# Routing, token lists and tile plan moved into the first shared half of the feed-forward, and a low part moved from VectorE to GpSimd

## The reference

```python
kv = einsum('bhil,bhjl->bijhl', k_, v_)
y = irfft(rfft(kv, n=2L) * rfft(ssm_kernel, n=2L))[..., :L]
out = einsum('bijhl,bhil->bjhl', y + kv * D, q_)
x = x + out
```

```python
scores = sigmoid(x @ router_w)                # 32 experts
group_scores = top-2 sum of (scores + bias) in each of 8 groups
keep 4 groups, take the top 8 experts; weights = scores / sum * 2.5
routed = sum over the 8 experts of w * (silu(x@gate) * (x@up)) @ down     # inner 512
shared = (silu(x @ sw_gate) * (x @ sw_up)) @ sw_down                      # inner 1024
out = x + routed + shared
```

## Time and profile before

| | us |
|---|---|
| median of 3 runs | 13680.2 (13676.1 to 13680.58) |
| profiled execution | 13610.97 |
| its span | 13609.1 |
| TensorE busy in the span | 13142.6 |

### The profile page before, as it was taken

How to read it: one execution, slowest core, us unless ns; L and a number is a source line. 1 busy time by engine, 2 the same in 40 slices (tenths; PEclk the granted TensorE clock), 3 DMA queues, 4 the chain that set the end, 5 groups by cost and what they waited for, 6 DMA issues and landing times.

```text
span 13609.1 us, 192445 instructions
## 1 busy us (share of the span) xinstructions
PE 13142.6 (97%) x59424; PEld 10914.0 (80%) x59425; DVE 5798.7 (43%) x6513; ACT 3143.2 (23%) x4072; POOL 6330.1 (47%) x6629
## 2 busy tenths in 40 slices
PE   8999995999999999999999999999898999999999
PEld 7888884888888888877888887877787888888887
DVE  6888785333333333343333333333334333333333
ACT  4444442111122111222122212222222112112111
POOL 5688886111444444444444444444444444444111
PEclk9999997999999999999999999999999999999999
DMA  3333333444444444455455545555555444444444
GB/s 120 118 115 111 115 115 91 135 128 127 113 114 110 103 107 104 115 146 127 98 114 132 115 97 127 125 135 142 141 115 159 98 97 114 97 97 103 128 128 120
DMA packets 876587, 1597.96 MB, mean 117 GB/s; under 512 B 169537, under 2 KB 518081, under 8 KB 850306
## 3 DMA queue, kind: packets, MB, share of 16 engines
q0 software_dynamic: 258560, 642.82, 23.1%
q1 hardware_dynamic: 134018, 600.31, 13.2%
q10 hardware_dynamic: 483840, 352.54, 10.4%
HBM read 995.66 MB, written 599.86 MB: 117 GB/s over the span
## 4 chain that ended last, share of the span: by engine, by line
PE 76%; DMA 2%; DVE 2%; issue 1%; ACT 1%; ACTq 0%; DVEq 0%; SPq 0%; POOL 0%
PE gps L1274 26%; PE ups L1274 26%; PE yps L1274 25%; DMA hsd<-hb 1%; DVE wlo L1199 1%; DMA hz<-hsd 1%; DMA raw<-in_w_gu_dram 0%; ACT whi L1143 0%; ACT xhi L1149 0%; DVE xlo L1199 0%; DVEq L991 0%; ACTq L1155 0%; DVE hp L1232 0%; ACTq L991 0%; DVE hb L1234 0%
## 5 line engine op out<-in xcount | busy, mean ns | idle before, releaser
L1112 POOL DMA_INDIRECT x2d<-yrow,yidx x544 | 945.7, 1738 | 3837.2 <-issue 1581.8
L1076 POOL DMA_INDIRECT xg<-xnd,xidx x2176 | 2156.7, 991 | 969.0 <-issue 473.2
L1199 DVE TENSOR_TENSOR xlo<-xt,xhi 128x1024 fp32r<-128x1024 f32 x672 | 822.5, 1224 | 3792.3 <-ACT xhi L1149 3792.3
L1274 PE MATMUL gps<-whi,xhi 128*128 128x512 f32 x5376 | 2098.2, 390 | 211.4 <-DVE xlo L1199 119.1
L1274 PE MATMUL ups<-whi,xhi 128*128 128x512 f32 x5376 | 2094.1, 390 | 0.0
L1274 PE MATMUL gps<-wlo,xhi 128*128 128x512 f32 x5376 | 2093.7, 389 | 0.0
L1274 PE MATMUL ups<-wlo,xhi 128*128 128x512 f32 x5376 | 2093.4, 389 | 0.0
L1274 PE MATMUL gps<-whi,xlo 128*128 128x512 f32 x5376 | 2093.3, 389 | 0.0
L1274 PE MATMUL ups<-whi,xlo 128*128 128x512 f32 x5376 | 2093.1, 389 | 0.0
L1274 PE MATMUL yps<-whi,hhi 128*128 128x512 f32 x5376 | 1667.6, 391 | 124.4 <-DVE wlo L1199 116.7
L1274 PE MATMUL yps<-wlo,hhi 128*128 128x512 f32 x5376 | 1662.3, 390 | 0.0
(11 more groups left out here) (149 smaller groups left out, 17382.3 us busy)
## 6 DMA issues: line engine op xcount, KB each, us to landing
hsd<-hb ACTq DMA_DIRECT2D x2688, 64.0 KB
hz<-hsd ACTq DMA_DIRECT2D x672, 256.0 KB, 2.7
raw<-in_w_gu_dram SPq DMA_DIRECT2D x136, 1024.0 KB, 7.2
raw<-in_w_dn_dram SPq DMA_DIRECT2D x68, 1024.0 KB, 6.9
xg<-xnd POOLq DMA_DIRECT2D x512, 128.0 KB
yrow<-x2d SPq DMA_DIRECT2D x128, 512.0 KB, 3.4
kT<-in_ctx_dram SPq DMA_DIRECT2D x64, 704.0 KB, 8.1
xg<-xnd,xidx POOLq DMA_INDIRECT x2176
```

Source lines behind the costliest of these rows:

```text
L1076: pool.indirect_dma_start(out=xg[i][:, q, :], out_offset=None, in_=quarters, in_offset=bass.IndirectOffsetOnAxis(ap=xidx[i][:, q:q + 1], a ...
L1112: pool.indirect_dma_start(out=acc, in_=yrow[i][:, :], in_offset=None, out_offset=bass.IndirectOffsetOnAxis(ap=yidx[i][:, 0:1], axis=0), co ...
L1199: return dve.tensor_tensor(dst, src, hi.bitcast(F32), ALU.subtract)
L1274: ins = pe.matmul(ps, rows, w[:, chunk, i * 512:(i + 1) * 512], start=first and n == 0, stop=last_one and n == 2)
```

## The change

- The routing leaves the mixing stage. `mix` keeps only the logits: ScalarE copies them into `lg`, 128 x 64 x 32, which stays in SBUF with `con` and `biasb`. `plan` is gone.
- In the mixing stage GpSimd makes the low part of group 3 as well, right after that of group 2; VectorE's `last_kv_lower` is gone. `xres` has two buffers.
- The feed-forward block begins right after mixing. Its SP loads the first x rows, the first weights, more x rows, and then goes through the first shared half with `pass_on`: x rows of the tile 3 ahead, store, wait, fetch. GpSimd loads no x rows in this half.
- ScalarE makes one sigmoid of all logits (128 x 2048) after the first weights are split.
- The 64 shared tiles are walked by `walk_routing` (tiles 0 and 1, then 8 rounds of 6 tiles, then tiles 50 to 59) and `walk_rest`. Each of a round's 6 tiles does one piece of routing on VectorE: `choose_groups`, `choose`, `weigh`, `count`, `assign`, `hand_over`. The piece stands between the addition to `yrow` and `hlo`. TensorE's two `ranks` matmuls stand in the third tile of the round, between gate/up and down. `plan_tiles` is the piece of tile 50.
- `assign` and `hand_over` fill the list entries in halves of 4 tiles (`match_half`). `assign` waits before its half for `place_free`, which GpSimd gives when the lists of the round before have landed.
- GpSimd goes through the 8 rounds of lists by itself, waiting for `placed` of each.

The diff, cut to its core:

```diff
-        xres = sb("xres", [P, L])
+        xres = [sb(f"xres{i}", [P, L]) for i in range(2)]
...
                 kv_lower(s, 2)
-                if isinstance(s.block, int) and s.block == BLOCKS - 1:
-                    list_tokens(s.block - 2, (2 * s.u, 2 * s.u + 1))
-                elif s.u < 7 and routes(s, s.u, 2):
-                    list_tokens(s.block - 2, ((0,), (1,), (2,), (3,), (4,), (5,), (6, 7))[s.u])
-                elif routes(s, 7, 2):
-                    free_place(s.block - 2)
+                kv_lower(s, 3)
...
-            def last_kv_lower(s):
...
-                if routes(s, 6, 1):
-                    count(s.block - 1)
...
-                if routes(s, 7, 1):
-                    assign(s.block - 1)
...
-                if g < GROUPS - 1:
-                    pe.wait_ge(kv_low, (GROUPS - 1) * n + g + 1)
-                else:
-                    pe.wait_ge(kv_low_last, n + 1)
+                pe.wait_ge(kv_low, GROUPS * n + g + 1)
...
-def plan(nc, A, keep):
...
+ROUNDS, PIECES, RANKS = NTILE // RB, 6, 2
+PLANNED = 2 + ROUNDS * PIECES
...
+def walk_routing(eng, tile, chain=None):
+
+
     for t in range(2):
         tile(Tile(t))
...
+    with eng.Fori(0, ROUNDS) as rnd:
+        if chain:
+            chain.restart(eng)
+        for u in range(PIECES):
+            tile(Tile(2, u, rnd * (PIECES // 2), rnd, u))
...
+    tile(Tile(PLANNED, piece=PIECES))
+    tile(Tile(PLANNED + 1))
+    pairs(eng, tile, PLANNED + 2, R0 - 4)
...
+            def pass_on(store, stored, first, end, ahead=0):
+
+                with sp.Fori(0, (end - first) // 2) as turn:
                     for i in range(2):
...
+                        n = first + 2 * turn + i
+                        if ahead:
+                            load_rows(n + ahead, (i + ahead) % 2)
+                        store(n, i)
+                        sp.wait_ge(stored[i], 16 * (first // 2 + turn + 1))
+                        fetch(n + 2, i)
...
+            load_rows(0, 0)
+            load_weights(sp, raw, w_ld, *expert_weights(A, 0), lambda unit: None)
+            load_rows(1, 1)
...
+            pool.sem_inc(place_free, 1)
+            with pool.Fori(0, ROUNDS) as rnd:
+                pool.wait_ge(placed, rnd + 1)
+                settle(pool, pool_turns)
+                for t in range(RB):
+                    list_tile(pool, lists, pair, place, t, listed)
+                pool.wait_ge(listed, 16 * RB * K * (rnd + 1))
+                pool.sem_inc(place_free, 1)
...
+            act.activation(lg[:, :, :], lg[:, :, :], ACT.Sigmoid).then_inc(scored, 1)
...
+                for t in range(RB):
+                    last = dve.max(top[:, t, :], key[:, t, :])
+                link(last)
+
+                dve.wait_ge(place_free, r + 1)
+                match_half(0)
...
+                if c.piece is not None:
+                    (choose_groups, choose, weigh, count, assign, hand_over, plan_tiles)[c.piece](c.rnd)
                 if c.on():
                     dve.wait_ge(h_hi, t + 1)
                     low(hlo[:, :, :].rearrange("p k (q s) -> p q k s", s=SQ), hz[:, :, :, :],
                         hhi[:, :, :].rearrange("p k (q s) -> p q k s", s=SQ)).then_inc(h_lo, 1)
...
+                if c.piece == RANKS:
+                    pe.wait_ge(chose, c.rnd + 1)
```

More of the change, by code:

```diff
@@ L240, in mix_and_route @@
         sd_out = sb("sd_out", [P, 3])
[L241 to L259, removed]
+        lg, con, biasb = keep["lg"], keep["con"], keep["biasb"]
         ident = con[:, C_ID:C_ID + P]
@@ L339, in step @@
                 if s.on(OUT):
-                    wait(sp, x2_st, 16 * s.n(OUT))
-                    sp.dma_start(xres[:, :], head_rows(x, s.n(OUT))).then_inc(r_ld, 16)
+                    i = s.slot(OUT)
+                    wait(sp, x2_st[i], 16 * s.half(OUT))
+                    sp.dma_start(xres[i][:, :], head_rows(x, s.n(OUT))).then_inc(r_ld[i], 16)
                 if s.on(FETCH):
@@ L700, in _ @@
             walk(dve, step, seq)
-            choose_groups(NTILE // RB - 1)
-            choose(NTILE // RB - 1)
-            count(NTILE // RB - 1)
-            assign(NTILE // RB - 1)
         @block.tensor
@@ L1044, in _ @@
                 sp.wait_ge(y_st[i], 16 * EXPERT_TILES // 2)
-            sums(store_sum, out_st)
+            for i in range(2):
+                fetch(i, i)
+            pass_on(store_sum, out_st, 0, NTILE - 2)
+            for i in range(2):
+                store_sum(NTILE - 2 + i, i)
             for i in range(2):
@@ L1118, in tile @@
                     load_list(c, 3)
-                if c.on(2):
+                if c.on(2) and c.part(2) != 0:
                     bring(c, 2)
@@ new lines, in choose @@
+            def choose(r):
+                link(dve.tensor_scalar(msk[:, :, :], msk[:, :, :], 0.0, None, ALU.add))
+                for t in range(RB):
+                    last = dve.max(top[:, t, :], msk[:, t, :])
+                link(last)
+                for t in range(RB):
+                    last = dve.match_replace(rep[:, t, :], top[:, t, :], msk[:, t, :], -3e38)
+                link(last)
+                dve.tensor_tensor(chosen[:, :, :], rep[:, :, :], msk[:, :, :], ALU.not_equal)\
+                    .then_inc(chose, 1)
+                dve.wait_ge(chose, r + 1)
@@ L1256, in tile @@
                     new_weights(dve, c, 0, split_dn)
-            for q in range(QUADS):
-                last = dve.tensor_copy(quad[:, q:q + 1], quarter[:, :])
-            last.then_inc(quad_ready, 1)
             x_turn(Tile(0), 0)
@@ L1264, in _ @@
             x_turn(Tile(0), 1)
-            walk_tiles(dve, tile)
+            for q in range(QUADS):
+                last = dve.tensor_copy(quad[:, q:q + 1], con[:, C_QUAD:C_QUAD + 1])
+            last.then_inc(quad_ready, 1)
+            dve.memset(cnt[:, :], 0.0)
+            dve.tensor_copy(tokf[:, :], con[:, C_TOK:C_TOK + RB])
+            walk_routing(dve, tile, seq)
+            dve.wait_ge(tab_ld, 16)
+            walk_rest(dve, tile)
         @block.tensor
```

450 lines of the change are left out of this document (204 added, 246 removed).

## The result

The changed kernel takes 13947.39 us (median of 4 runs, 13938.39 to 13958.61), the kernel before 13680.39 in the same session (4 runs, 13676.1 to 13695.64): 1.0194 times, interval 1.0176 to 1.0211. Forecast were 13540 us. It is 267 us slower instead of 140 faster, and outside of every rival's case.

What follows compares the result with a forecast made beforehand. TensorE, busy 97% of the span, was taken to bound the kernel. Mixing -69, start of feed-forward -109, ranks matmuls +7 and wait for lists +31 gave -140 us, from 13680.2 to 13540, range 13495 to 13600.

Steps and rivals of the forecast that it cites:

- What bounds the kernel: Whole kernel: TensorE bounds it, busy 97% of the span; in mixing it loses 14.1 us per eight heads to routing.
- Mixing without routing: Mixing stage, heads 8 to 62: without routing each head takes 32.63 us, a gain of 69 us.
- The low part on GpSimd: Mixing stage: the added 2.70 us a head hides in over 10 us of GpSimd's idle time; cost 0.
- From mixing to the first tile: Start of feed-forward: first matmul comes 23 us after the barrier instead of at 2365.9, a gain of 109 us.
- Pieces of routing, ranks matmuls: First shared half: VectorE's pieces fit in 8.7 us of room, cost 0; the ranks matmuls cost TensorE 7 us.
- The wait for the lists: First shared half: VectorE waits 6.7 us in assign for GpSimd's lists, costing TensorE 4.4 us in seven rounds, 31 us.
- The upper bound, 165 us in all: Wait for the lists at most: GpSimd's round takes 97.5 us, TensorE idles 14.4 us a round, plus 9.2 of clock.
- The exclusion by VectorE, the third case: Long stall in the shared half: VectorE's exclusion or late landings make GpSimd's round 91 us or more; 13593 to 13674; chance 0.24.
- no room before `hlo`: Shared half: routing pieces stand wholly on TensorE's path, 248 us with clock, giving 13757 us; chance 0.04.
- these 69 us: Profiled execution against the median of runs: the median is 69 us above, and the same difference was assumed after the change.
- 13509: Rival without a stall in the shared half: lists land in time, -171 us, giving 13509 us; chance 0.19.

Runs made afterwards that it cites:

- e1: The changed kernel without its 512 list transfers, so lists stay blank and routed tiles compute with other rows; 13435.03 us.
- e7: The kernel before with only the last low part of each head moved from VectorE to GpSimd; 13720.11 us, ratio 1.0031.
- e12: The changed kernel with each round's 64 indirect list transfers replaced by 64 plain GpSimd transfers of the same pieces to fixed rows; 13513.68 us.
- e17: The changed kernel without h's way through HBM in all tiles, and without row loads and yrow's store and fetch in the first shared half; 13847.19 us.
- e9: The changed kernel with each of the 512 list transfers making 16 writes instead of 128; 14000.16 us.
- e15: The changed kernel with room for four rounds' places and shares, rounds written out, and a GpSimd pause after every second list transfer; 13551.23 us, ratio 0.991.

## Why the prediction was wrong, by its steps

*What bounds the kernel.* Right: `e1`, with all pieces in the shared half, keeps TensorE busy 1207.11 of 1210 us.

*Mixing without routing.* Right, if 5 us short: heads 8 to 62 take 2135.94 - 368.94 = 1767.0 us, forecast 1762.0; a gain of 64.2 for 69.2.

```profile
368.94 1.21 DVE L521 TENSOR_TENSOR xres<-xres,ps 128x1024 f32<-128x1024 f32 x1
...
2135.94 1.21 DVE L521 TENSOR_TENSOR xres<-xres,ps 128x1024 f32<-128x1024 f32 x1
```

*The low part on GpSimd.* Cost nothing here, as forecast. Alone it is a loss of 0.3% (`e7`), but with the slow stretches in it; beneath mixing the changed kernel has no list transfers that could bring them.

*From mixing to the first tile.* Right: the first matmul is at 2190.14, forecast 2188. That it is within 2 us is partly luck: the last logits come at 2170.1, over 5 us later than forecast, and from there it takes 20 us instead of 23.

```profile
2169.93 0.20 ACT L431 ACTIVATE lg<-pss 128x32 f32<-128x32 f32 x1 [3.71 <-PE pss L613]
...
2190.14 0.79 PE L1246 MATMUL gps<-whi,xhi 128*128 128x512 f32 x1 [20.25 <-DVE xlo L1162]
```

*Pieces of routing, ranks matmuls.* Right: these and the two steps before give a span of 13469 - 31 = 13438 us without the wait; `e1` had 13433.3.

*The wait for the lists.* This is the step that failed. It priced the 64 transfers by what they take of GpSimd, and by VectorE's wait at their end: 4.4 us of TensorE's time a round, 31 us in all, where the runs show 512. What the transfers do to the other engines while they are issued it put at nothing. GpSimd's side of it was right, 81.1 us from first to last issue in the first round. But they took 64 us a round of TensorE's time while they were issued, by slowing its instructions and not by a wait. VectorE's wait for the place hardly came about, since VectorE itself was slowed: in the window 2250 to 3460 it is GpSimd that waits for VectorE, 699.0 us in 7 times. The upper bound, 165 us in all, looked only at the same wait, made longer. (Its 4.4 us a round for a busy VectorE come out at 4.0 by its rows, which changes nothing.) The exclusion by VectorE, the third case, doesn't show either: with VectorE busy 11.27 of 20 us at the start of the burst, GpSimd still issues 16 transfers. The rival *no room before `hlo`* had the right sign and the wrong mechanism: the pieces have room, as `e1` shows.

*Could the trace have shown it?* The recorded execution of the kernel before misled: a burst of 64 such transfers, 1.27 us apart, begins at 2159.3 beneath mixing, and TensorE stays full beside it until its own work ends at 2210. Its window of the first 40 us:

```profile
2160.00:2200.00 40.00, 39.77 (x212) 33.93 (x211) 26.75 (x27) 5.04 (x8) 30.55 (x32) 1.00 0.17 41
```

But that execution (13611.0 us, clock 0.986) was 69 us quicker than the median of the timed ones and 62 us quicker than the quickest (13673 to 13683 for 11, clock 0.983 to 0.984). I took these 69 us for a difference that the change would carry along. It did not: for the kernel after, profile (13950.5) and median (13947.4) agree, and for `e7` (13721.2, 13720.1). A slow stretch in that last burst, as in `e7`, would account for them. Heads 61 and 62 are 99.7 us apart in `e7` and 32.2 in the recorded kernel before, 67.5 us more, and up to head 61 `e7` is 42.4 us behind it, which is what the medians differ by. This is argued, since no trace of a 13680 us execution of the kernel before was at hand. First `e7`, then the kernel before (its head 62 is in the earlier trace rows):

```profile
2209.27 1.21 DVE L580 TENSOR_TENSOR xres<-xres,ps 128x1024 f32<-128x1024 f32 x1
...
2308.97 1.21 DVE L580 TENSOR_TENSOR xres<-xres,ps 128x1024 f32<-128x1024 f32 x1
```

```profile
2166.84 1.21 DVE L582 TENSOR_TENSOR xres<-xres,ps 128x1024 f32<-128x1024 f32 x1
```

It also means that the size forecast for a kernel without a wait for lists, 13509, was 74 us too high: `e1` took 13435.

*What stays open.* Why indirect transfers closely behind one another slow the other engines' instructions. Shown: it needs indirect transfers (`e12`) and no other transfer (`e17`); it comes with 1.15 to 1.3 us a transfer (`e9`, the change) and not with 1.62 and a pause after every second (`e15`); and from the start of a round's burst it takes some 11 to 15 of them in a row, 13 to 19 us. Their writes' number and place, the loops and the operands' addresses don't matter. That isn't enough for it, since the recorded execution of the kernel before has 50 us of such transfers without. Not tested are even paces between 1.3 and 1.6 us without pauses, and in the shared half bursts of more than eight and fewer than 64. The Trainium skill (DMA: Bandwidth & Descriptors, "SWDGE vs HWDGE vs iDMA") says that GpSimd writes the descriptors of its transfers into rings in SBUF, that VectorE can lock it out of doing so, and that transfers issued from SyncE and ScalarE never touch this path and are immune to that interference. What is seen here is another interference: VectorE is busy 0.69 of 60 us in the stretch, GpSimd's transfers keep their pace, and SyncE's own issue went from 0.44 to 1.93 us each. The skill (NOTIFIC — the notification-queue block, "Overflow: three behaviours, one of which stalls the engine") says that the block that writes out the records of a trace can, in one of its modes, hold an engine up until software has drained them. All times here are of executions with such records; no run tells whether the stretches come from the instructions or from their being recorded.

## What to carry to other kernels

Price a moved burst by what it does to every engine beside it, and not only by its own length: look for the same burst, at the same pace and as long, beside a saturated TensorE, and in more than one execution. It paid here to spread GpSimd's small indirect transfers: a pause after every second one and room for four rounds turned a 1.9% loss into a 0.9% gain. And where the recorded execution is quicker than every timed one, something that the others pay may be missing in it; no step should be priced at nothing on its word alone.

## What the runs showed of the hardware

- After some 11 to 15 indirect transfers 1.27 us apart, TensorE's weight loads and matmuls start 0.70 to 1.40 us after one another and wait for nothing, and an issue of SyncE takes 1.93 us instead of 0.44, mostly until the burst ends or pauses; at 1.62 us on average, with a pause after every second, there was none. It isn't so in every execution: the recorded one of the kernel before had none.
- While TensorE ran single matmuls with gaps of 2.2 us, its granted clock stood at or near the lower level, 1.2 GHz: 0.54 over 2351 to 2411, and 0.50 over 40 us of `e9`.
- Plain transfers of GpSimd of the same pieces are issued 0.53 us apart and cause no slow stretch (`e12`).
